# Asking for the second adjacency group ahead of the stores of the normalised rows

## What is computed

```
h    = layernorm(x)
q, k, v = h @ Wq.T, h @ Wk.T, h @ Wv.T
mask = adj.T
attn = softmax(where(mask, q @ k.T, -1e30))      # 0 where mask is False
x    = x + attn @ v
g    = layernorm(x)
p    = softmax(g @ W_router); the two largest of 8 are kept and scaled to sum 1
x    = x + sum over the two chosen experts e of p_e * (relu(g @ W1[e] + b1[e]) @ W2[e] + b2[e])
```

## Time and profile before

| | before |
|---|---|
| median of 3 runs | 870.7 us (870.02 to 871.3) |
| the profiled execution, its own time | 869.89 us |
| its span, first to last instruction | 868.2 us |
| mean granted TensorE clock | 0.888 of full speed |
| busy: PE / DVE / ACT / POOL | 705.0 / 574.5 / 455.6 / 426.1 us |
| first gather to last gather (L502) | 41.4 to 253.9 us |
| PE's first expert matmul (L1415) in the chain that ended last | 417.47 us |

### The profile page before, as it was taken

One profiled execution on the slowest core, in us unless ns is written; L12 is line 12 of the kernel. 1 busy time (PEld: TensorE's weight loads), 2 busy tenths in 40 slices (PEclk: granted clock), 3 DMA queues, 4 the chain that ended last, 5 costly groups with the idle time before them and its releaser, 6 DMA issues.

```text
span 868.2 us, 22858 instructions
## 1 busy us (share of the span) xinstructions
PE 705.0 (81%) x6398; PEld 640.5 (74%) x6399; DVE 574.5 (66%) x2058; ACT 455.6 (52%) x1286; POOL 426.1 (49%) x482
## 2 busy tenths in 40 slices
PE   2549999999987704461899999999999999999994
PEld 1448888888877404450798998889889899898993
DVE  8745766667866667526676866758676766766554
ACT  2636556655565303332556656556555656556563
POOL 2077777777750287775144343343334334444443
PEclk9559999999997755565899999999999999999997
DMA  9884345541211023566532231422333142122121
GB/s 291 265 214 120 86 110 143 134 124 46 79 43 49 27 84 100 162 228 226 185 109 74 95 122 56 150 79 89 115 118 107 61 158 73 51 73 62 53 64 34
DMA packets 89587, 96.73 MB, mean 111 GB/s; under 512 B 10427, under 2 KB 78533, under 8 KB 89404
## 3 DMA queue, kind: packets, MB, share of 16 engines
q1 hardware_dynamic: 70860, 61.46, 24.1%
q0 software_dynamic: 18672, 34.66, 12.5%
HBM read 82.25 MB, written 30.33 MB: 130 GB/s over the span
## 4 chain that ended last, share of the span: by engine, by line
PE 36%; issue 6%; DMA 5%; DVE 4%; POOL 2%; DVEq 1%; ACT 1%; POOLq 0%; SPq 0%; ACTq 0%
PE psE L1426 11%; PE psH L1415 6%; PE psH L1417 6%; PE psH L1416 6%; PE psE L1428 5%; DMA acc<-out,tok_next 4%; PE psX L1402 2%; POOL out L586 1%; DVE y_out L1122 1%; DMA out<-y_out,tok_now 1%; DVE h_lo L1146 1%; DVE x_lo L1100 0%; ACT x_hi L1617 0%; POOL acc L577 0%; DMA x_in<-expert_in 0%
## 5 line engine op out<-in xcount | busy, mean ns | idle before, releaser
L1631 ACT ACTIVATE z_all<-psH,b1T 128x256 f32<-128x256 f32 x296 | 142.6, 482 | 161.3 <-PE psH L1417 160.6
L1426 PE MATMUL psE<-w_parts,h_hi 128*128 128x512 f32 x552 | 209.6, 406 | 2.6 <-DVE h_lo L1146 1.9
L502 POOL DMA_INDIRECT nbr<-xn_rows,idx x160 | 165.0, 1031 | 83.7 <-issue 81.3
L1146 DVE TENSOR_TENSOR h_lo<-z_all,h_hi 128x256 fp32r<-128x256 f32 x296 | 122.7, 424 | 83.6 <-ACT h_hi L1632 82.9
L1415 PE MATMUL psH<-x_hi,w_hi 128*128 128x256 f32 (+1 forms) x592 | 166.1, 281 | 11.1 <-issue 7.6
L1417 PE MATMUL psH<-x_hi,w_lo 128*128 128x256 f32 (+1 forms) x592 | 165.8, 280 | 0.0
L1416 PE MATMUL psH<-x_lo,w_hi 128*128 128x256 f32 (+1 forms) x592 | 165.6, 280 | 0.0
L1428 PE MATMUL psE<-w_parts,h_lo 128*128 128x256 f32 x552 | 154.9, 281 | 0.0
L1632 ACT ACTIVATE h_hi<-psH,b1T 128x256 fp32r<-128x256 f32 x296 | 142.1, 480 | 0.0
L586 POOL DMA_INDIRECT out<-y_out,tok_now x74 | 77.2, 1043 | 114.3 <-DVE y_out L1122 98.2
L1415 PEld LDWEIGHTS psH<-x_hi,w_hi 128*128 128x128 f32 x592 | 112.2, 190 | 22.6 <-issue 15.0
(11 more groups left out here) (335 smaller groups left out, 1168.5 us busy)
## 6 DMA issues: line engine op xcount, KB each, us to landing
w_raw<-in_L_ffn_W SPq DMA_DIRECT2D x16, 1024.0 KB, 5.4
x_in<-expert_in SPq DMA_DIRECT2D x38, 260.0 KB
adj_even<-in_adj SPq DMA_DIRECT2D x4, 2048.0 KB
late<-in_adj SPq DMA_DIRECT2D x4, 2048.0 KB
x_all<-in_x SPq DMA_DIRECT2D x4, 1024.0 KB, 9.3
xn_rows<-z_all SPq DMA_DIRECT2D x4, 1024.0 KB
out<-x_all SPq DMA_DIRECT2D x4, 1024.0 KB, 4.9
expert_in<-pad_row SPq DMA_DIRECT2D x8, 390.0 KB, 4.8
```

What stands on the lines that cost most here:

```text
L502: pool.indirect_dma_start(nbr[:, u * K + k, :], None, xn_rows, bass.IndirectOffsetOnAxis(ap=idx[:, u, k:k + 1], axis=0), bounds_check=ROW0 ...
L1146: dve.tensor_tensor(h_lo[:, hc, :], h_f[:, hc, :], h_hi[:, hc, :].bitcast(F32), ALU.subtract).then_inc(hl_ready, 1)
L1426: pe.matmul(psE[:, q, :], h_hi[:, hc, m], w2_parts[:, b, hc].rearrange("p s c -> p (s c)"), start=(hc == 0), stop=False)
L1631: act.activation(h_f[:, hc, :], psH[:, hc % 4, 0:T], ACT.Relu, bias=b1T[:, e * HC + hc:e * HC + hc + 1])
```

## The change

SP issues the load of group 1 right behind that of group 0, before the four stores and the block. Its old place, behind the wait for `xn_stored`, falls away. Nothing else changes; the loop for groups 2 to 7 stays.

```diff
             sp.dma_start(adj_in[0], adj_u8[:, :, 0:GT * P]).then_inc(adj_loaded[0], 16)
+            sp.dma_start(adj_in[1], adj_u8[:, :, GT * P:2 * GT * P]).then_inc(adj_loaded[1], 16)
 
             for i in range(4):
...
-            next_group(1, 1)
             with sp.Fori(1, NG // 2) as i:
                 next_group(i * 2, 0)
                 next_group(i * 2 + 1, 1)
```

## The result

The changed kernel takes 874.62 us (median of four runs, 874.4 to 874.87) against 870.41 for four runs of the kernel before: a ratio of 1.0047, 95% interval 1.0030 to 1.0064. It is slower by 4.2 us. The measured time lies inside the range on record, 869.6 to 875.6, but near its upper end and outside the likeliest band, 870.9 to 872.9. "Slower", which came out, had a chance of 0.43, "the same" 0.50.

What follows compares the result with a forecast made beforehand. Bound by stores, gathers, score, diag and weigh of tile 0, then the PE and ACT clockwork. Stores 4.8 us later, less the gathers' relief, gave +1.5: 870.7 + 1.5 = 872.2 us, range 869.6 to 875.6.

Steps and rivals of the forecast that it cites:

- The chain: Before tile 0's weigh: stores landed, gathers issued, gathers landed, score, diag, weigh; group 1 a side branch with 4.92 us spare.
- the rivals: Alternative outcomes: delay paid in full 875.5 (0.2), one more half-clock stretch 873.9 (0.23), stores get in anyway 867.9 (0.07).
- The stores' landing: On SP's queue: group 1 adds 7.2 us, empty stretches absorb 2.4, so stores land 4.8 us later, about 45.0.
- The lower bound of 3.8: Least delay of the stores' landing, if all stores ran at 382 GB/s: +3.8 us, landing at 43.0.
- the gathers' relief: Tile 0's gathers meet only group 2: fifth gather starts at 51.7 and lands at 54.9, before 6.5 us after its start.
- The term "+1.5": Net delay of tile 0's score, at 55.0 instead of 53.52, passed on to the whole kernel: +1.5 us.
- my two bounds (+1.0 and +4.8): Tile 0's score delay: +1.0 if the fifth gather lands 2.7 us after its start, +4.8 if held 6.5.
- POOL's floor: At the attention's end: POOL's later start means the end cannot come sooner than 4.8 - 3.75 = +1.0 us.
- The rival of one more half-clock stretch: PE's clock at 0.50 once more, 1.66 us: 873.9; chance 0.23, shared with tile 5's 0.7 on top.
- The page's rule of turns between queues: DMA engines alternate queues packet by packet, so SP's queue hardly holds tile 0's gathers: score near 54.5, +1.0.

Runs made afterwards that it cites:

- the two pure delays: Kernel before with POOL's first gather held by extra fills, load order unchanged: longer delay ratio 1.0031 (2.7 us slower), shorter 1.0018 (1.6 us slower).
- the kernel with the hold taken away: Changed kernel, but group 2 is asked for only once the codes of tile 5 are done: 872.15 us, ratio 1.0017 to the kernel before.
- the second session: The changed kernel unaltered, run again beside fresh runs of the kernel before: 874.68 us, median of 10 runs, ratio 1.0037.

## Why the prediction was right, and where it was not

**The chain was right.** PE's wait of 5.61 us for group 1 was worth nothing, as argued: it became idle time ahead of the same diag. Stores, gathers, score, weigh set the rest, and the two pure delays show the one-for-one behind it. The time itself was met less well: 3.2 and 4.2 us slower against a forecast of 1.5. The range held it because it left room for the rivals, and two misses in the sum partly cancel, as follows.

**The stores' landing: +4.8 forecast, +4.2 measured.** The queue ran without a gap, as forecast, but the stores went at 379 to 385 GB/s and not at 337. The lower bound of 3.8, worked out with 382, was the better guide.

**The step that failed is the gathers' relief.** I took the fifth gather to land at 54.9, near its lower bound, because a held gather would be let go 8.7 us after group 2 was asked for, at 54.2. Most of group 2 was through by then; the queue rows of the changed kernel for 51 to 54 us and, below, for 54 to 57 show it:

```profile
q1 hardware_dynamic: 1201, 0.61, 80.2%
q0 software_dynamic: 188, 0.23, 28.9%
```
```profile
q0 software_dynamic: 191, 0.24, 27.8%
q1 hardware_dynamic: 74, 0.04, 4.6%
```

But the last 74 packets were not nothing. They came until 55.4, and group 2, asked for at 44.84, landed 11.1 us later, at 55.9:

```profile
DMA to landing us min/median/max: 11.1/11.1/11.1
```

The term "+1.5" is 4.8 + 3.3 - 6.64, the last being the 53.52 - 46.88 of the earlier trace rows; measured it is 4.2 + 5.25 - 6.64 = +2.8. The relief was 1.9 us too large, the stores' landing gave 0.6 of it back, and the forecast came out 1.3 us too low. The price lay between my two bounds (+1.0 and +4.8); the mechanism was right and the size was off. What the first comparison shows beyond 2.8, 1.4 us, is within its interval.

**POOL's floor** (+1.0 in the prediction; 4.2 - 3.75, about +0.5, with the measured start) showed itself in the kernel with the hold taken away, whose last score waited for a gather. In the changed kernel it did not decide: the last score waited for the query copy, as before:

```profile
262.94 0.42 DVE L700 CUSTOM_DVE_ANT_0 prod<-q_sb,nbr 128x256 f32<-128x256 f32 x1 [2.07 <-ACT q_sb L1513]
```

**The rival of one more half-clock stretch** came true in the first profile, with 1.66 us, but the second session's profile again has three stretches and the delayed kernels two, and their times follow the shift all the same. It is part of the spread of single executions and not shown to be a steady cost of the change.

**The page's rule of turns between queues** (the Trainium skill, "DMA: Bandwidth & Descriptors", "Queues, rings and completion order") would, as the prediction read it, have let the score start near 54.5, or near 53.9 from the measured start of the fifth gather. With a load beside the gathers it started at 56.32, without one at 53.80. The measurement decides: here a full load queue holds a gather for some 2.5 us more. Why it does, no run here shows.

## What to carry to other kernels

A wait that stands large in the profile is worth removing only if what follows it does not wait for something later: here PE's 5.61 us for a load only became part of the wait for the diag. Look instead for the transfer that nobody needs yet and that runs beside the one on the path; holding back group 2 by one wait brought 3.8 us (2.4 to 5.3), while moving group 1 forward cost 3 to 4. And a load moved ahead of a store cost nothing here as far as the queue had empty stretches there.

## What the runs showed of the hardware that was not expected

Stores back to back ran at 379 to 385 GB/s, where the stretch of two stores in the kernel before had shown 337. An issue on SP took up to 9.37 us, right behind 3 MB of `x` and group 0, at no cost that the rows show: the queue stayed full meanwhile. And identical runs of the kernel before spread from 868.12 to 873.76 us in two sessions of 24 and 33 runs; single profiles of one kernel put the half-clock stretches of TensorE at quite different places, so a profile of each is not enough to compare kernels that differ by 2 us.
